# Two woven drains, a four-tile last piece and three counts of warm-up products in a four-stage graph and expert kernel

## The reference, cut to what matters

```
x = x + gnn0(layernorm(x), adj)      # 4 heads, sigmoid scores, normalised by degrees
x = x + ffn0(layernorm(x))           # each token goes to 2 of 8 experts
x = x + gnn1(layernorm(x), adj)      # a = u / sum(u), u = mask * exp(e + f); a @ h
x = x + ffn1(layernorm(x))           # each batch goes to 2 of 8 experts

# the end of ffn1, for every token
out = sum over the 2 chosen experts of w * y_expert
out = (z - mean(z)) * rsqrt(var(z) + 1e-5) * gamma + beta,   z = out + x
```

## Time and profile before

| what | value |
|---|---|
| median of 3 runs (lowest, highest) | 725.49 us (725.46, 728.45) |
| profiled execution | 725.08 us |
| its span | 723.1 us |
| mean granted TensorE clock | 0.958 |
| busy: TensorE matmul, VectorE, ScalarE, GpSimd | 633.0, 532.2, 469.3, 344.3 us |
| first TensorE work of the second stage's blocks (line 1441) | 313.65 us |
| first expert product of the fourth stage (line 2233) | 591.47 us |
| last expert product ends | 709.53 us |
| last `yout` ends | 720.81 us |

### The profile page before, as it was taken

How to read it: one execution, slowest core, us unless ns; L and a number is a source line. 1 busy time by engine, 2 the same in 40 slices (tenths; PEclk the granted TensorE clock), 3 DMA queues, 4 the chain that set the end, 5 groups by cost and what they waited for, 6 DMA issues and landing times. The chain is left out here.

```text
span 723.1 us, 18595 instructions
## 1 busy us (share of the span) xinstructions
PE 633.0 (88%) x5438; PEld 534.7 (74%) x5438; DVE 532.2 (74%) x2362; ACT 469.3 (65%) x1284; POOL 344.3 (48%) x520
## 2 busy tenths in 40 slices
PE   2788998988998969879999999996899698999992
PEld 1555665665665637769999999995788677999992
DVE  7899999999999978534444444444899931778798
ACT  1878988888889742247666666672267747676660
POOL 1124444767667757614545454455532106756530
PEclk9999999999999977889999999997999889999997
DMA  5339322432321102445544444316993002112121
GB/s 157 102 104 191 101 77 73 129 101 89 98 88 60 64 27 52 151 141 154 135 117 126 144 144 128 102 51 122 226 235 141 1 0 60 31 59 60 32 68 49
DMA packets 75844, 72.15 MB, mean 100 GB/s; under 512 B 7793, under 2 KB 64818, under 8 KB 74978
## 3 DMA queue, kind: packets, MB, share of 16 engines
q1 hardware_dynamic: 61954, 50.28, 24.9%
q0 software_dynamic: 11200, 13.35, 7.5%
q10 hardware_dynamic: 2592, 7.34, 3.6%
HBM read 44.39 MB, written 26.55 MB: 98 GB/s over the span
## 5 line engine op out<-in xcount | busy, mean ns | idle before, releaser
L1515 ACT ACTIVATE hT<-psum,b1blk 128x128 f32<-128x128 f32 x364 | 103.8, 368 | 54.1 <-PE psum L1452 54.1
L1628 POOL DMA_INDIRECT expert_outputs<-y_rows,y_at x91 | 86.9, 955 | 98.0 <-DVE y_rows L1601 94.4
L1452 PE MATMUL psum<-xinT,w1blk 128*128 128x128 f32 x728 | 98.0, 278 | 0.1
L1473 PE MATMUL psum<-f_w,hT 128*128 x728 | 96.3, 276 | 0.0
L1452 PEld LDWEIGHTS psum<-xinT,w1blk 128*128 128x128 f32 x728 | 90.0, 195 | 0.7 <-ACT xinT L1505 0.4
L1473 PEld LDWEIGHTS psum<-f_w,hT 128*128 128x128 f32 x728 | 88.4, 192 | 0.2
L1582 DVE TENSOR_SCALAR w1blk<-f_w 128x256 f32 x182 | 47.3, 301 | 46.8 <-issue 43.6
L836 DVE TENSOR_TENSOR adj_h<-psum,adjT 128x1024 f32<-128x1024 f32 x64 | 75.2, 1215 | 0.6 <-ACT psum L612 0.6
L612 ACT ACTIVATE psum<-psum 128x1024 f32<-128x1024 f32 x64 | 64.1, 1007 | 14.3 <-PE psum L362 14.3
L1167 POOL DMA_INDIRECT pair_rows<-rows,row_of x64 | 63.1, 987 | 19.5 <-issue 15.8
L1601 DVE TENSOR_TENSOR y_rows<-psum,b2wide 128x128 f32<-128x128 f32 x91 | 26.5, 292 | 52.4 <-PE psum L1473 47.3
(11 more groups left out here) (324 smaller groups left out, 1492.9 us busy)
## 6 DMA issues: line engine op xcount, KB each, us to landing
adj_in<-in_adj_dram SPq DMA_DIRECT2D x32, 256.0 KB, 3.5
adjT_scratch<-adjT SPq DMA_DIRECT2D x32, 256.0 KB, 2.9
adjT<-adjT_scratch SPq DMA_DIRECT2D x6, 1024.0 KB, 5.1
xin<-pair_rows SPq DMA_DIRECT2D x91, 64.5 KB, 2.0
b2wide<-b_of_blocks ACTq DMA_DIRECT2D x10, 512.0 KB
xres<-in_x_dram SPq DMA_DIRECT2D x16, 256.0 KB, 3.7
xres<-expert_outputs POOLq DMA_DIRECT2D x6, 512.0 KB, 8.7
out_dram<-yout SPq DMA_DIRECT2D x6, 512.0 KB, 3.4
```

Of the source, the lines that this page charges most:

```text
L1452: ins = nc.tensor.matmul(psum[:, 2 + u, lo:lo + P], w1blk[:, u, k, c * P:(c + 1) * P], xinT[:, u, :], start=True, stop=True)
L1473: ins = nc.tensor.matmul(psum[:, 6 + n % 2, 0:D], hT[:, u, k, c, :], flat[:, bass.ds(places[k] + (HID + c * D), D)], start=(k == 0 and c = ...
L1515: ins = nc.scalar.activation(hT[:, u, k, c, :], psum[:, 2 + u, lo:lo + P], ACT.Gelu, bias=b1blk[:, c, k, n:n + 1])
L1628: pool.indirect_dma_start(y_dram[:, :], bass.IndirectOffsetOnAxis(ap=y_at[:, n % Y_AT:n % Y_AT + 1], axis=0), y_rows[:, u, :], None).then_ ...
```

## The change

It has five parts.

1. In the first drain `keep_busy(26)` becomes `keep_busy(30)` and `keep_busy(24)` becomes `keep_busy(18)`.
2. In the drain of gnn1 the loop that issued all root steps before the residual is gone; in slots 6 and 7 the roots are woven with the residual, as in the slots before.
3. At the start of ffn1 `keep_busy(LOAD_BANK, 16)` becomes `keep_busy(LOAD_BANK, 5)`.
4. The last two pieces of one batch each become one piece of two batches (4 tiles).
5. In the tail the rest of the third last piece is woven with the first steps of the piece of batches 28 and 29, three steps of which stand between the inputs of batches 30 and 31; what is left of it is woven with the last piece.

```diff
--- before.py
+++ after.py
@@ -590,12 +590,12 @@
             gates_of_two(NB - 6)
             pe.wait_ge(s_xd, NB)
             pe.wait_ge(s_const2, CONST2)
-            keep_busy(26)
+            keep_busy(30)
             rank(IN_DRAIN + 1, L1)
             transpose_rows_late(NB - 4)
             transpose_rows_late(NB - 3)
             gates_of_two(NB - 4)
-            keep_busy(24)
+            keep_busy(18)
             rank(IN_DRAIN + 2, L2)
             transpose_rows_late(NB - 2)
             transpose_rows_late(NB - 1)
@@ -2021,9 +2021,6 @@
                 steps = iter(())
                 if have(s + 2) or have(s - 1):
                     steps = solve_steps(s + 2 if have(s + 2) else None, s - 1 if have(s - 1) else None)
-                if not have(s + 2):
-                    for _ in steps:
-                        pass
                 if have(s):
                     add_residual(s, steps)
                 for _ in steps:
@@ -2140,7 +2137,7 @@
         CAPACITY = float(-(-NB * NN * 5 // (4 * NE)))
         FIRST_W1 = 2
 
-        LN_BATCHES = [GB] * (NG - 2) + [2, 2, 2, 1, 1]
+        LN_BATCHES = [GB] * (NG - 2) + [2, 2, 2, 2]
         IN_EXPERTS = "HID times the number of an expert, found among eight"
         LN_PARTS = [(2 * sum(LN_BATCHES[:i]), 2 * n) for i, n in enumerate(LN_BATCHES)]
 
@@ -2181,7 +2178,7 @@
                     nc.tensor.matmul(psum[:, bank, 0:P], ident[:, :], before[:, :], start=True, stop=True)
 
             phase3_done(pe)
-            keep_busy(LOAD_BANK, 16)
+            keep_busy(LOAD_BANK, 5)
             last = NG - 1
             pe.wait_ge(s_rstd3, 2 * last + 1)
             for j in range(GB):
@@ -2470,18 +2467,23 @@
                 quota = 8 if n == GB else 11
                 for j in range(n):
                     add_input(LN_PARTS[i][0] // 2 + j)
-                    for _ in range(quota):
+                    for _ in range(quota if (i, j) != (len(LN_BATCHES) - 2, n - 1) else 0):
                         next(steps, None)
+                if i == len(LN_BATCHES) - 2:
+                    break
                 for _ in steps:
                     pass
                 steps = finish_steps(i, chF)
-            for _ in range(6):
-                next(steps, None)
+            ahead = finish_steps(len(LN_BATCHES) - 2, ch, 2 * GB - 4)
+            for _ in steps:
+                next(ahead, None)
+            add_input(NB - 2)
+            for _ in range(3):
+                next(ahead, None)
             add_input(NB - 1)
-            final = finish_steps(len(LN_BATCHES) - 1, ch, LN_PARTS[-2][1])
-            for _ in steps:
-                next(final, None)
-            for _ in final:
+            for _ in finish_steps(len(LN_BATCHES) - 1, chF):
+                next(ahead, None)
+            for _ in ahead:
                 pass
 
         def ffn1_gpsimd(pool):
```

## The result

The change made the kernel faster by about what was said, and somewhat more. The median went from 725.58 us (725.46 to 728.45, 4 runs beside it) to **715.57 us** (714.79 to 715.96, 4 runs): ratio 0.9886, 95% interval 0.985 to 0.9921. Forecast were 718.4 us and a range of 715.0 to 721.8. The profiled execution took 715.96 us; its span is 714.2 us where it was 723.1, so 8.9 us are to be accounted for. Lines behind the deleted three (L2024 to L2026 of before) are numbered three lower.

The account below looks back on a forecast made before the run. VectorE's work was taken to bound the end, and short chains over three engines the drains. From 725.08 us, 2.0 (first drain), 2.3 (second) and 2.5 (tail) gave 718.3, said as a median of 718.4; range 715.0 to 721.8.

Parts of the forecast that it names:

- two cases: First drain, rank of route 7: 1.4 us won with the clock of before, 2.7 if the clock stays up.
- the term of 2.0: First drain: the shorter second run makes the rank early, and the first block's work comes 2.0 us earlier.
- rival (b): First drain's gain not passed on, as landing sends or first row loads are bound otherwise: 720.3 us; chance 0.10.
- the 5 needs the weave: Second drain: the 5 constant products and the woven roots need each other; 2.3 us won at the row sums.
- the weave's gain on ScalarE (1.4): Second drain: woven roots let ScalarE start the last group at 579.4 instead of 580.78 us, 1.4 earlier.
- the 0.5 that the prediction gave as its bound: Second drain: if the row sums run at half clock, taking twice 1.84 us, 0.5 us of gain remains.
- a possible upside: First expert product, 3.39 us at 0.42 a pass: 1.5 us more could be had, or lost on the next eight.
- Rival (a): Second drain: with 11 products fewer, half clock lasts through sums, transposes and first experts: 721.6 us; chance 0.12.
- The sign that the prediction named for being wrong: Second drain: a granted clock of 0.50 behind the row sums, one of three signs named.
- Rival (c): Tail: the last piece of four tiles and the 256 KB eat most of the gain: 720.0 us; chance 0.06.
- (e): Last layer's expert stage: half clock holds, slower than before, about 735 us from five batches on; chance 0.02.
- (d): All three drains give their upper ends, 2.7, 4.6 and 3.0 us: some 715 us; chance 0.10.

Follow-up runs that it names:

- the kernel with 26 and 24: The changed kernel with both first-drain `keep_busy` counts set back, 30 to 26 and 18 to 24: 716.58 us, ratio 0.9893.
- 2 place products: The changed kernel with GpSimd's `add_beta` of the last group early, plus `keep_busy(PLACE_BANK, 6)` cut to 2: 729.54 us, ratio 0.9876.
- the two later comparisons: The changed kernel run again, unedited, beside the kernel before in two later sets: 714.91 us (0.989) and 731.35 us (0.9907).
- the three other kernels run there: Edits of the changed kernel: last pieces in turn, only the last two woven (735.35 us); `add_beta` early (727.9); that plus `keep_busy(PLACE_BANK, 2)` (729.54).

## Why the prediction was right, and where it was not

**First drain: right up to the rank of route 7; beyond it, not shown.** The prediction gave two cases, with the clock lost (1.4) and kept (2.7), and took 2.0. The clock was kept, and the rank stands behind `upto`, as its sum for that case had it: second run near 4.2 us (4.26), idleness 1.5 (1.69). At the rank it is 2.74 us, forecast 2.7. What it took back for half clock behind the idleness, up to 1.3 us, did not come in this trace, where the clock stayed at 1.00 to 300; in three of five executions with these counts the clock did fall there, and in one it cost 1.6 us. It credited both numbers; at the rank the 30 is enough. The step that is not borne out is the next one, that the first block's work comes earlier by as much. The trace has 2.9 us from the rank of route 6 on, or 2.23 counted from the span's start, but the kernel with 26 and 24 has all but 0.5 of it with its rank as late as before. So that the term of 2.0 came out near is luck in part, and rival (b) stands open. GpSimd's idleness was used up as forecast (2.22 us before, 0.30 now, 2.15 with 26 and 24).

**Second drain: 2.3 forecast, 2.9 measured.** Half of the rest is the end of group 6's last transposes: 578.5 by the prediction, 576.23 in the trace, which had `den` of group 5 1.98 us earlier, so 0.3 of it is real. The other half is overlap, which the sum did not have: the constant products begin 0.2 us before the transposes end, and the sums 0.16 before theirs do. Slot 6's woven block, 562.73 to 566.35 + 0.17, is 3.79 us, forecast 3.8; the ten passes are 2.26, forecast 2.2. That with 16 products nothing is won held; that the 5 needs the weave did not. The fault was to take the weave's gain on ScalarE (1.4) for what the 5 lives on, where the sums without it begin only 0.5 us later. And the 2.9 is that of an execution whose sums ran at full clock: with half clock, in five of eleven, it is 1.3, against the 0.5 that the prediction gave as its bound for that.

**First expert product: 1.5 us that stood only as a possible upside.** This is the largest miss. The prediction read 3.39 us for eight passes, knew 1.9 as their price at full clock, and left the difference out of the sum, since half clock behind a shorter fill seemed as likely to stay as to go. In this execution the clock was back at 585, ahead of the product. Whether this belongs to the change is not settled: twelve executions of kernels with some part of the second drain changed show 1.89 us, but of the kernel before only one was profiled, so how often it has 3.39 is not known. Rival (a), half clock through the sums and the first experts, held in its first part in six of twelve executions with 5 products (sums of 3.41 to 3.58 us), in the second only with 2 place products. The sign that the prediction named for being wrong, a clock of 0.50 behind the row sums, did show (582 to 585), and went with only 0.45 us: that much the choice gave back, as the place products ran at half clock and ended at 585.07, while `second` had been there since 584.27.

**Tail: 2.5 forecast, 2.55 measured.** 10.96 us against 11.0, and 2.3 us to landing for 256 KB instead of 1.8. Prices per step from the chain of waits were enough; nothing hidden came out. Rival (c) fell.

**Expert stage and rivals.** 0.5 us earlier in the first batches, up to TensorE's third output product, which before waited 0.36 us for VectorE's first input; what shifted that input is open. (e) did not happen. (b) is not excluded: with 26 and 24 a late rank did not make the blocks late. (d), all drains at their upper ends (2.7, 4.6 and 3.0; about 715), is close to what this trace shows: 2.9 in the first drain, 2.9 and 1.5 in the second and the first expert product, 2.55 net in the tail. The measured 715.57 lies nearer to it than to the forecast, and 0.6 us from the range's lower end.

**The sum.** 8.9 in the trace, 6.8 forecast: +0.9 first drain, +0.6 second, +1.5 expert product, +0.5 expert stage, 0 tail, less 0.7 + 0.25 + 0.45 that the first stage, the second block stage and the choice gave back. Terms below a us are of the order in which executions of one kernel differ; what the runs establish is 10.0 us between the medians of the result, 8.3 and 7.4 in the two later comparisons (ratios 0.9886, 0.989, 0.9907; each interval lies below 1). Of that the tail is the part that the times show as well: undoing it cost 3.3 us (12 runs against 6).

## What to carry to other kernels

Try a fill in the idleness that precedes the clock's fall: with four products more in those 1.1 to 1.4 us the clock was up at the next run in six of six executions, without them in one of four, and the twenty-four products behind it had then delayed the rank. Count more than one trace before crediting it, for the next idleness lost the clock as well, and the time showed no gain. Where short dependent steps end a kernel, merge the last two pieces before weaving them: one chain of roots fewer is 2.3 us (0.5 of it lost to the larger last transfer), weaving 0.8. And read the longest of a group of equal instructions, not only their mean: one of 64 that takes 2443 ns among 345 names a collision with the engine that runs at that moment.

## What was not expected of the hardware

- The kernel before spreads by 10 us over its runs on one chip (718.33 to 728.15), and its time goes with the run's mean granted clock, 0.951 to 0.970 (correlation -0.79 in 19 runs, -0.68 in 28). Differences of a us or two between medians of six runs say nothing; stretches between two named steps in two traces repeat to some 0.1 us where the clock is the same and no DMA lies between them.
- On a third chip the kernel before took 738.79 us and the change 731.35. In the first drain TensorE there stood for "issue" between the four transposes behind the rank of route 6, up to 1.11 us before one of them, and from rank to rank it took 14.37 us instead of 9.10; the three other kernels run there showed 14.2 to 14.9. It is not TensorE alone: in all four ScalarE's `xh1T` behind those transposes started after 3.93 to 4.10 us of idleness and VectorE's `pos` behind the rank after 3.36 to 3.59, and with 2 place products the four transposes stood without a gap and ended at 289.19, while ScalarE went on only at 292.78. What made them wait is open: the profile puts most of these waits down to "remote" and names no engine. TensorE, then VectorE, of the changed kernel:

```profile
291.38 0.31 PE L538 MATMUL psum<-ident,rows 128*128 128x128 f32 x1 [1.11 <-issue]
292.78 0.37 PE L538 MATMUL psum<-ident,rows 128*128 128x128 f32 x1 [1.10 <-issue]
...
295.55 5.75 PE L343 MATMUL psum<-before,ident 128*128 128x128 f32 x36
```

```profile
293.07 0.39 DVE L970 TENSOR_TENSOR pos<-psum,filled 128x224 f32<-128x224 f32 x1 [3.45 <-remote]
```

- One `yout` on VectorE took 2443 ns for the 345 of its kind, beside an addition on GpSimd of 2.43 us. A mean of the group hides it. Five root steps of 0.16 us took 1.94 to 1.95 in the same way.
